# One DMA request moved forward in SyncE's program: the query and key weights of the attention steps

## Chip, cores, metric

The kernel runs on one core of one Trainium2 chip. The metric is device time in microseconds. Times are medians of several executions; every number about a single instruction is from one profiled execution.

## The reference, cut to what matters

The input is 1024 tokens of width 256 (2 sequences of 512). The output is x + A(xn) + F(xn), with xn the layer norm of x. A is a gated delta-rule attention with 16 key heads and 32 value heads. F is a causal softmax attention with 16 heads and then a mixture of 16 experts (4 chosen for each token) beside a shared expert. The change lies in F's softmax attention:

```python
x = rmsnorm(hidden_states, ln1_w)
q = jnp.einsum('bsh,dh->bsd', x, q_w).reshape(b, s, NH, QHD)[..., :NOPE]
kv = jnp.einsum('bsh,dh->bsd', x, kv_w)
k = kv[..., :NH * NOPE].reshape(b, s, NH, NOPE)
v = kv[..., NH * NOPE:NH * (NOPE + VD)].reshape(b, s, NH, VD)
scores = jnp.einsum('bqnd,bknd->bnqk', q, k) * scale
p = jax.nn.softmax(jnp.where(causal, scores, -1e9), axis=-1)
attn_out = jnp.einsum('bsd,hd->bsh', jnp.einsum('bnqk,bknd->bqnd', p, v).reshape(b, s, -1), o_w)
```

## The kernel before

The program has three stages, one after the other: F's attention (to about 500 us), the experts (to about 675 us), and A (the rest). Each engine has its own instruction list, and the engines meet at semaphores.

**The attention steps.** There are B * PAIRS = 16 steps, k = 0 to 15: 2 sequences times 8 pairs of heads. The weights of a step are three tiles, each with a single buffer: `wqk` (queries and keys, 512 KB), `wv` (values, 256 KB) and `wo` (output, 256 KB). TensorE works ahead by one step in part. Its order in step k is:

1. `project_v(k)` (L517), which reads `wv`. From its end on (`s_v` at 2k+2) `wv` is free.
2. `project_qk(k + 1, 0, 2)` (L502), the queries of the *next* step, for two heads. It waits for `s_ldq`, which the landing of `wqk` of step k+1 raises, and for the copies of the values out of PSUM (`s_vE`, DVE's `take_v`, L1459).
3. For i = 0 and 1: turn the probabilities (L594, waits for DVE's `s_prob`, L1622), then `project_qk(k + 1, 2 + i, 3 + i)`, the keys of the next step (L502 again). At the end of the second of them `s_qk` stands at 4(k+1)+4 and `wqk` is free.
4. Probabilities times values (L606), then `scores(k + 1, 0)` (L527).
5. The output projection (L628), which reads `wo` and raises `s_o`, then `scores(k + 1, 1)` (L527).

In steps 9, 10 and 12 some router work is put between (L535, L545, L553 to L559). Beside this DVE masks the scores, takes row maxima and scales the probabilities, and ScalarE exponentiates them and copies PSUM to SBUF.

**SyncE's list** asks for all transfers from memory and waits in order, so whatever stands behind a wait is late with it. In step k it waits for `s_qk` at 4k+4 and asks for `wqk` of step k+1 (L314), waits for `s_v` and asks for `wv` of step k+1 (L316), waits for `s_o` and asks for `wo` of step k+1 (L323), and then asks for the large transfers that the expert stage needs: in steps 0 to 7 two writes of zeros of 1 MB each to `xs_dram` (`clear_rows`, L305), in steps 8 to 15 the weights of one expert, 352 KB and 176 KB (`load_expert`, L308 and L309). In step 0 two stores of gate tables (L320) and a small write of zeros (L326) stand between. All of them go through one DMA queue.

Of the kernel before, what the change touches and what calls it, by code (L numbers as in the profile page):

```python
# [7 lines left out]
B, S, H = 2, 512, 256  # L8
# [14 lines left out]
PAIRS = NH // 2  # L23
# [20 lines left out]
def build(nc, d, out, debug=None):  # L44
# [9 lines left out]
    with ExitStack() as ctx:  # L54
# [3 lines left out]
        def sem(name):  # L58
            return ctx.enter_context(nc.semaphore(name))
# [16 lines left out]
        def early(name, shape, dt=F32):  # L76
            return early_ctx.enter_context(nc.sbuf_tensor(name, shape, dt))
# [32 lines left out]
        wqk = early("wqk", [P, 2, HK, 2 * P])  # L110
# [145 lines left out]
        sm = {n: sem(n) for n in names}  # L256
# [22 lines left out]
        def _(sp):  # L279
            dma = sp.dma_start  # L280
# [21 lines left out]
            def clear_rows(c):  # L302

                rows = xs_dram[c * CAP:(c + 1) * CAP].rearrange("(p m) h -> p m h", p=P)
                dma(rows, zeros[:].unsqueeze(1).broadcast_to([P, CAP // P, H])).then_inc(sm["m_zero"], 16)  # L305

            def load_expert(e):
                dma(we13[:, e, :], d["we13"][e].rearrange("p k n -> p (k n)")).then_inc(sm["m_we"], 16)  # L308
                dma(we2[0:IH, e, :], d["we2"][e].rearrange("p k n -> p (k n)")).then_inc(sm["m_we"], 16)  # L309

            for k in range(B * PAIRS):
                if k + 1 < B * PAIRS:
                    sp.wait_ge(sm["s_qk"], 4 * k + 4)
                    dma(wqk[:], d["wqk"][(k + 1) % PAIRS]).then_inc(sm["s_ldq"], 16)  # L314
                    sp.wait_ge(sm["s_v"], 2 * k + 2)
                    dma(wv[:], d["wv"][(k + 1) % PAIRS]).then_inc(sm["s_ldv"], 16)  # L316
                if k == 0:
                    sp.wait_ge(sm["s_gate_a"], 8)
                    for rows, table in ((grow_dram, growT), (erow_dram, erowT)):
                        dma(rows, table[:]).then_inc(sm["s_st"], 16)  # L320
                if k + 1 < B * PAIRS:
                    sp.wait_ge(sm["s_o"], 2 * k + 2)
                    dma(wo[:], d["wo"][(k + 1) % PAIRS]).then_inc(sm["s_ldo"], 16)  # L323
                if k == 0:
                    sp.wait_ge(sm["s_eps"], 3)
                    dma(xs_dram[E * CAP:], zeros[:]).then_inc(sm["m_zero"], 16)  # L326
                if k < 8:
                    clear_rows(2 * k)
                    clear_rows(2 * k + 1)
                else:  # L330
                    load_expert(k - 8)
# [1831 lines left out]
```

## Time and profile before

| | |
|---|---|
| median of 3 executions | 1696.54 us |
| lowest and highest of them | 1686.31 and 1699.68 us |
| the profiled execution, its own time | 1692.79 us |
| its span, from the first to the last instruction | 1691.0 us |
| mean granted TensorE clock | 0.966 |
| TensorE (PE) busy | 1556.0 us, 92% of the span |
| VectorE (DVE), ScalarE (ACT), GpSimd (POOL) busy | 1111.0, 785.5 and 438.8 us |
| moved by DMA | 136.88 MB, 81 GB/s on average |

The profile names an instruction by its line in the kernel. A busy TensorE says only that it had work, since a slower clock makes the same work last longer. A float32 matmul of 512 columns stands as two records. Consecutive matmul records overlap by about 0.16 us, so the length of a run of them is best taken from start to start. Names are cut to their common part: `we` holds the probabilities in DVE's and ScalarE's rows, and `act_t` holds keys, values and attention outputs.

### The profile page before, as it was taken

To read this page: it belongs to the slowest core of one execution; us is meant where nothing else is said; L and a number is where in the kernel's file an instruction comes from. 1 tells how busy PE (TensorE), PEld (TensorE's weight loads), DVE (VectorE), ACT (ScalarE), POOL (GpSimd) and SP (SyncE) were. 2 spreads that over 40 slices of the span, in tenths; PEclk is the share of its full clock that TensorE was granted. 3 is DMA by queue.
4 is the path that set the end of the run, shared out by engine and by line. 5 is a ranking of instruction groups with operands and counts; after the bars stand their busy time and mean duration, and the time that the engine had idled before them with its cause. 6 is when DMAs were issued, how large, how long until landed. Compare 5 with 4: busy or idle time off the path is not lost.

```text
span 1691.0 us, 29153 instructions
## 1 busy us (share of the span) xinstructions
PE 1556.0 (92%) x10922; PEld 1088.7 (64%) x10922; DVE 1111.0 (66%) x2442; ACT 785.5 (46%) x1692; POOL 438.8 (26%) x277
## 2 busy tenths in 40 slices
PE   5898889899997999659999999999999999999987
PEld 3556556566664676337776876776687677667756
DVE  4524324446536232377898898889888888988875
ACT  3433333434341333344665556465555646554641
POOL 0000000000304000523454263445415333531410
PEclk9999999999999899879999999999999999999999
DMA  2322322211333332513323331432333133233200
GB/s 94 103 75 85 140 75 98 90 60 55 125 86 99 107 107 79 142 50 69 98 62 80 91 87 49 103 97 62 79 83 79 41 94 86 57 67 84 59 10 32
DMA packets 225051, 136.88 MB, mean 81 GB/s; under 512 B 160976, under 2 KB 196304, under 8 KB 224912
## 3 DMA queue, kind: packets, MB, share of 16 engines
q1 hardware_dynamic: 221840, 126.62, 27.3%
q0 software_dynamic: 3072, 8.39, 1.5%
q8 instruction: 89, 1.46, 0.4%
q14 instruction: 50, 0.41, 0.1%
HBM read 94.85 MB, written 35.91 MB: 77 GB/s over the span
## 4 chain that ended last, share of the span: by engine, by line
PE 74%; issue 10%; DMA 6%; DVE 5%; SPq 2%; ACT 2%; POOL 1%; POOLq 1%; ACTq 0%; DVEq 0%
PE ps L502 7%; PE ps L909 7%; PE ps L808 7%; PE ps L827 6%; DMA wqk<-in_wqk 6%; PE ps L606 4%; PE ps L628 3%; PE ps L746 3%; PE ps L848 3%; PE ps L879 3%; PE ps L756 3%; PE ps L858 2%; PE ps L878 2%; PE ps L835 2%; PE ps L594 2%
## 5 line engine op out<-in xcount | busy, mean ns | idle before, releaser
L502 PE MATMUL ps<-xrT,wqk 128*128 128x512 f32 x256 | 134.8, 665 | 45.0 <-DMA wqk<-in_wqk 41.2
L1276 ACT ACTIVATE vs<-ps 128x256 f32<-128x256 f32 x128 | 49.2, 384 | 260.2 <-PE ps L848 256.0
L2024 POOL TENSOR_TENSOR qg<-qT,Ebc 128x1024 f32<-128x1024 f32 x32 | 75.0, 2364 | 357.1 <-PE ps L879 357.1
L1484 DVE TENSOR_TENSOR ps<-ps,causal_neg 128x128 f32<-128x128 f32 x128 | 37.4, 292 | 189.1 <-PE ps L527 189.1
L1701 DVE SCALAR_TENSOR_TENSOR cv<-ps,cw,cv 128x1022 f32<-128x1022 f32 (+2 forms) x96 | 122.6, 1279 | 28.1 <-ACT cv L1223 24.2
L808 PE MATMUL ps<-xnT,gv 128*128 128x512 f32 x256 | 121.7, 619 | 12.0 <-DVE cv L1701 11.5
L909 PE MATMUL ps<-wout,xT 128*128 128x256 f32 x512 | 128.8, 396 | 2.2 <-DVE total L1811 2.2
L1712 DVE SCALAR_TENSOR_TENSOR cv<-ps,cw,cv 128x1022 f32<-128x1022 f32 (+2 forms) x96 | 122.5, 1277 | 5.9 <-ACT cv L1255 3.6
L1811 DVE SCALAR_TENSOR_TENSOR total<-ps,rr,total 128x256 f32<-128x256 f32 x256 | 118.8, 480 | 10.0 <-POOL rr L2030 3.0
L827 PE MATMUL ps<-xnT,gz 128*128 128x512 f32 x256 | 121.1, 597 | 2.4 <-DVE MT L1745 2.2
L502 PEld LDWEIGHTS ps<-xrT,wqk 128*128 128x128 f32 x256 | 50.7, 213 | 100.4 <-issue 48.7
L1154 ACT ACTIVATE we<-ps,bias 128x128 f32<-128x128 f32 (+3 forms) x128 | 65.8, 526 | 106.0 <-DVE bias L1488 106.0
L909 PEld LDWEIGHTS ps<-wout,xT 128*128 128x128 f32 x512 | 93.3, 192 | 28.2 <-issue 12.6
L808 PEld LDWEIGHTS ps<-xnT,gv 128*128 128x128 f32 x256 | 47.5, 196 | 86.6 <-issue 73.6
L2008 POOL TENSOR_TENSOR dec<-dec,cb 128x1024 f32<-128x1024 f32 x32 | 60.1, 1898 | 166.3 <-DVE cb L1734 134.8
L1966 POOL TENSOR_SCALAR mean<-ssq 128x4 f32<-128x4 f32 x2 | 0.4, 192 | 362.9 <-ACT junk L1138 362.9
L879 PE MATMUL ps<-AT,vs 128*128 128x128 f32 x512 | 91.1, 275 | 0.0
L848 PEld LDWEIGHTS ps<-vs,PT 128*128 128x128 f32 x512 | 66.7, 194 | 26.1 <-issue 15.7
L1223 ACT ACTIVATE cv<-ps,cw 128x1024 f32<-128x1024 f32 x32 | 35.7, 1115 | 94.5 <-PE ps L756 62.0
L1994 POOL TENSOR_TENSOR dec<-dec,e_neg 128x1024 f32<-128x1024 f32 x32 | 75.4, 2377 | 16.1 <-DMA dec<-grow_dram 16.1
L878 PE MATMUL ps<-qg,St 128*128 128x128 f32 x384 | 74.4, 275 | 0.0
L527 PE MATMUL ps<-act_t,we 128*128 128x128 f32 (+3 forms) x256 | 74.3, 434 | 0.0
(256 smaller groups left out, 3581.4 us busy)
## 6 DMA issues: line engine op xcount, KB each, us to landing
xs_dram<-zeros SPq DMA_DIRECT2D x16, 1024.0 KB, 6.4
dec<-grow_dram SPq DMA_DIRECT2D x32, 512.0 KB, 4.8
Ebc<-erow_dram SPq DMA_DIRECT2D x32, 512.0 KB, 5.0
wqk<-in_wqk SPq DMA_DIRECT2D x16, 512.0 KB, 6.7
xn<-xs_dram SPq DMA_DIRECT2D x47, 128.0 KB, 2.0
ys_dram<-yg SPq DMA_DIRECT2D x47, 128.0 KB, 1.8
we<-in_we SPq DMA_DIRECT2D x16, 352.0 KB
wv<-in_wv SPq DMA_DIRECT2D x16, 256.0 KB, 4.6
```

The lines of the kernel that those rows point to most:

```text
L502: last = mm(ps[:, 6 + j % 2, :], wqk[:, i, c, w * P:(w + 1) * P], xrT[:, c, at:at + S], start=(c == 0), stop=(c == HK - 1))
L808: last = mm(ps[:, (Y, X)[r] + b, :], gv[:, k, r * D:(r + 1) * D], xnT[:, k, b * S:(b + 1) * S], start=(k == 0), stop=(k == HK - 1))
L827: last = mm(ps[:, X + b, :], gz[:, k, r * D:(r + 1) * D], xnT[:, k, b * S:(b + 1) * S], start=(k == 0), stop=(k == HK - 1))
L848: last = mm(ps[:, b, r * D:(r + 1) * D], PT[:, r * NT + 4 * b + m, :], vs[:, r, 4 * b + m, :], start=True, stop=True)
L878: mm(dst, St[:, m % 2, b * R + r, :], qg[:, r, t, :], start=True, stop=False)
L879: last = mm(dst, vs[:, r, t, :], AT[:, h % 2, r, t, :], start=(m == 0), stop=True)
L909: last = mm(ps[:, output_bank(t), r * H:(r + 1) * H], xT[:, r, t * P:(t + 1) * P], wout[:, r, :], start=True, stop=True)
L1701: ins = stt(row, pair(bank)[:, :, 0:S - k], cw[:, f, i, TAPS - 1 - k:TAPS - k], row, ALU.mult, ALU.add)
L1712: ins = stt(row, pair(bank)[:, :, 0:S - k], cw[:, n, 2 + r, TAPS - 1 - k:TAPS - k], row, ALU.mult, ALU.add)
L1811: ins = stt(total[:, t, :], ps[:, output_bank(t), r * H:(r + 1) * H], rr2[:, r, t:t + 1], total[:, t, :], ALU.mult, ALU.add)
L1994: tt(dec[:, r], dec[:, r], e_neg[:].unsqueeze(1).broadcast_to([P, NT, P]), ALU.add).then_inc(fl["g_self"], 1)
L2024: tt(qg[:, r], qT[:], Ebc[:, r], ALU.mult).then_inc(fl["g_qg"], 1)
```

## The change

SyncE asks for the `wqk` of step k+2 in step k, as soon as the last projection of step k+1 has read the buffer, ahead of its wait for `s_o`. The large expert transfers of a step now stand behind that request. The request for step 1 stands ahead of the loop. The same transfers are made, from the same engine, in another order; no other engine's list is touched.

```diff
+            sp.wait_ge(sm["s_qk"], 4)
+            dma(wqk[:], d["wqk"][1]).then_inc(sm["s_ldq"], 16)
             for k in range(B * PAIRS):
                 if k + 1 < B * PAIRS:
-                    sp.wait_ge(sm["s_qk"], 4 * k + 4)
-                    dma(wqk[:], d["wqk"][(k + 1) % PAIRS]).then_inc(sm["s_ldq"], 16)
                     sp.wait_ge(sm["s_v"], 2 * k + 2)
                     dma(wv[:], d["wv"][(k + 1) % PAIRS]).then_inc(sm["s_ldv"], 16)
+                if k + 2 < B * PAIRS:
+                    sp.wait_ge(sm["s_qk"], 4 * k + 8)
+                    dma(wqk[:], d["wqk"][(k + 2) % PAIRS]).then_inc(sm["s_ldq"], 16)
                 if k == 0:
                     sp.wait_ge(sm["s_gate_a"], 8)
                     for rows, table in ((grow_dram, growT), (erow_dram, erowT)):
```

## Rows read from the trace of the kernel before

**Rows 1.** The page's second part: granted TensorE clock in 40 slices of 42 us.
```profile
PEclk9999999999999899879999999999999999999999
```
**Rows 2.** TensorE's waits, first from 84 to 328 us, then from 328.5 to 485 us.
```profile
PE ps L502 <- DMA wqk<-in_wqk: 35.5, 8, 5.5
...
PE ps L502 <- DMA wqk<-in_wqk: 5.7, 6, 2.0
```
**Rows 3.** Timeline of TensorE in step 2, one of those with zero writes.
```profile
106.90 3.62 PE L517 MATMUL ps<-wv,xrT 128*128 128x256 f32 x16
114.53 5.40 PE L502 MATMUL ps<-xrT,wqk 128*128 128x512 f32 x8 [4.01 <-DMA wqk<-in_wqk]
119.76 1.25 PE L594 MATMUL ps<-ident,we 128*128 128x128 f32 x10
120.86 1.88 PE L502 MATMUL ps<-xrT,wqk 128*128 128x512 f32 x4
122.58 1.25 PE L594 MATMUL ps<-ident,we 128*128 128x128 f32 x10
...
131.86 3.62 PE L628 MATMUL ps<-wo,act_t 128*128 128x256 f32 x16
135.31 2.32 PE L527 MATMUL ps<-act_t,we 128*128 128x128 f32 x8
137.47 3.62 PE L517 MATMUL ps<-wv,xrT 128*128 128x256 f32 x16
```
**Rows 4.** TensorE, first and last value projection between which the stalls lie; later steps.
```profile
74.92 3.62 PE L517 MATMUL ps<-wv,xrT 128*128 128x256 f32 x16
...
340.09 1.04 PE L535 MATMUL ps<-ident,xn 128*128 128x128 f32 x8
...
366.60 1.86 PE L545 MATMUL ps<-wgate,xrT 128*128 128x16 f32 x16
...
419.94 0.79 PE L559 MATMUL ps<-keep,chunk_ones 128*128 128x48 f32 x6
...
436.25 3.70 PE L502 MATMUL ps<-xrT,wqk 128*128 128x512 f32 x8 [2.03 <-DMA wqk<-in_wqk]
...
483.21 3.62 PE L517 MATMUL ps<-wv,xrT 128*128 128x256 f32 x16
```
**Rows 5.** Timeline of SyncE's requests in one round: start, time to issue.
```profile
104.94 0.33 SPq L323 DMA_DIRECT2D wo<-in_wo  x1
105.31 1.26 SPq L305 DMA_DIRECT2D xs_dram<-zeros  x2
106.62 1.79 SPq L314 DMA_DIRECT2D wqk<-in_wqk  x1
110.55 0.33 SPq L316 DMA_DIRECT2D wv<-in_wv  x1
```
**Rows 6.** The chain that ended last: transfers of the weights in steps 2 and 13.
```profile
106.62 7.87 DMA wqk<-in_wqk
...
430.55 5.66 DMA wqk<-in_wqk
```
**Rows 7.** Groups by line and shape, 83 to 330 us: the projection's records.
```profile
L502 PE MATMUL ps<-xrT,wqk 128*128 128x512 f32 x131 | 76.8, 729 | 35.8 <-DMA wqk<-in_wqk 35.8
```
**Rows 8.** Windows of TensorE; of all engines in the last row. PEclk, DMA share and GB/s end each.
```profile
78.50:328.70 250.20, 214.45 (x801) 0.93 0.29 102
328.70:485.00 156.30, 150.90 (x625) 1.00 0.21 72
...
700.00:1650.00 950.00, 922.52 (x8287) 658.33 (x8284) 803.86 (x1638) 528.04 (x988) 380.20 (x218) 0.98 0.30 73
```
**Rows 9.** Timeline of DVE behind the value projection of step 14, which ends at 460.95.
```profile
461.15 0.69 DVE L1459 COPY act_t<-ps 128x512 f32<-128x512 f32 x1 [0.93 <-PE ps L517]
...
461.96 1.27 DVE L1622 TENSOR_SCALAR we<-we,prec 128x128 f32<-128x128 f32 x4
...
463.35 1.27 DVE L1622 TENSOR_SCALAR we<-we,prec 128x128 f32<-128x128 f32 x4
```

## The prediction

> **What bounds the kernel now.** I read the page first: TensorE is busy 92% of the span, so time can be won only where it idles or where its clock is low. The slices of the granted clock [rows 1] dip in slices 6 to 8, at about 210 to 335 us, inside the attention stage, and nowhere else below nine tenths. The table of waits then names the idle time of that stage: from step 1 on TensorE waits for one thing alone, the landing of `wqk`, 14 times, 35.5 us in eight waits of steps 1 to 8 and 5.7 us in six waits of steps 9 to 14 [rows 2]. Together that is 41.2 us.
>
> The timeline shows where. In step 2 the value projection starts at 106.90 and lasts 3.46 us (that is what the output projection of the same form takes from its start at 131.86 to the next start at 135.31), so TensorE is free at 110.36. It then stands still to 114.53, when `wqk` has landed [rows 3]. SyncE's list says why: `wqk` is asked for only at 106.62, behind `wo` and two zero writes of 1 MB, which were asked for at 104.94 and 105.31 [rows 5]. Its transfer then takes 7.87 us behind the zero writes, but 5.66 us behind one expert's weights [rows 6]. That is the difference between the two kinds of waits in [rows 2]. The chain that ended last runs through this transfer in each of these steps, so the wait is on the path.
>
> **Second cost of the wait: the clock.** The first projections behind a long wait are slow. Eight records of L502 need 5.23 us from start to start in step 2 (114.53 to 119.76), while four need 1.72 us a little later (120.86 to 122.58), so eight should need 3.44 us [rows 3]. In step 13, behind a wait of 2.03 us, the eight records are shown with 3.70 us instead of 5.40 [rows 3, 4]. The granted clock fits: 0.93 on average in steps 1 to 8, 1.00 in steps 9 to 14 [rows 8]. A mean of 0.93 is a mixture of the two levels, 2.4 and 1.2 GHz, and the lower one follows each wait of 4 us and more. The Trainium skill, "TensorE: Matmul & The Clock Gate", Part 1, says the same in general: the low clock is the default, and activity releases it; by that rule this cost goes with the wait.
>
> The sum of it comes from one row. From 83 to 330 us L502 has 131 records with 76.8 us of busy time [rows 7]: eight steps of 16 and three of the ninth. At full clock a step shows 3.60 + 1.88 + 1.88 = 7.36 us (3.44 plus the overlap of 0.16; 1.88 as in [rows 3]), so eight steps and three records (3 x 0.43 + 0.16) need 58.9 + 1.45 = 60.3 us. The low clock costs 76.8 - 60.3 = 16.5 us. In steps 9 to 14 the remainder (3.70 against 3.60) is 6 x 0.10 = 0.6 us.
>
> **The change, part by part.**
> - *The request for the next `wqk` moves ahead.* It now goes out when the last projection of step k+1 has read the buffer, which in step 2 would be about 125.4 (the L594 group that starts at 122.58 takes 1.10, and four records of L502 behind it 1.72). It is needed at the end of the next value projection, 137.47 + 3.46 = 140.93, so 15.5 us later [rows 3]. The transfer takes at most 7.87 us as shown, now with nothing large ahead of it. So at least 7 us are to spare, and all 14 waits go: 41.2 us, plus the overlap of 0.16 us that each wait row leaves out (110.36 is the true end, the row counts from 110.52), 2.2 us.
> - *The low clock behind the waits goes too*: 16.5 + 0.6 us.
> - *A new wait in SyncE's list* (`s_qk` at 4k+8). Queued behind it are the wait for `s_o` with `wo`, the zero writes or expert weights, and the next `wv`. The wait ends before L628 of the same step has even begun, and SyncE would have waited for L628 anyway, so none of them moves. In step 0 the two table stores of L320 come later within the step; they are read only in stage A. Cost 0; the lower bound is 0, since `wo` cannot go out before `s_o` in either kernel. The upper bound is one more issue of 1.79 us [rows 5] where nothing waits for it.
> - *`wv` is now the first request behind the zero writes.* It is asked for behind `s_v` (110.55, 5.2 us behind the first zero write) and is needed a full step later, some 24.6 us. Even with 7.87 us of transfer it has 16 us to spare. The skill's page "DMA: Bandwidth & Descriptors", section "Queues, rings and completion order", says that each DMA engine takes the descriptors of a ring in order, which makes `wv` the one that inherits the place of `wqk`; the rows here show that it can afford it.
> - *Zero writes and expert weights*: same requests, same place relative to L628. They come sooner in absolute time, as TensorE does.
>
> **What is late next.** Without the wait L594 follows 3.44 us behind L517. I take the slack from step 14, where L517 ends at 460.95. DVE copies the second half of the values until 461.84; the second projection needs it at 460.95 + 1.72 = 462.67: 0.8 us to spare. The first set of probabilities is scaled at 461.96 + 1.27 = 463.23, needed at 464.39: 1.16 us. The second is scaled at 464.62, needed at 467.21: 2.6 us [rows 9]. All three follow from the end of L517 and do not depend on the wait taken away, so no new wait comes up. The margin is thin, though, and it is the first thing to look at.
>
> **The sum, two ways.** By terms: 41.2 + 2.2 + 16.5 + 0.6 = 60.5 us. By periods: from the value projection of step 1 at 74.92 to that of step 15 at 483.21 are 408.3 us for 14 steps [rows 4]. A step without wait is 17.71 (119.76 to 137.47) + 3.46 + 3.44 = 24.6 us [rows 3], 14 of them 344.5; the router's pieces add 0.9 in step 9, 1.7 in step 10 and, with their two leading records, about 0.9 in step 12 [rows 4]. 408.3 - 344.5 - 3.5 = 60.3. Both agree. The later stages start from TensorE's own progress, so they shift as a whole.
>
> The profiled execution took 1692.79 us; less 60.4 is 1632.4. It is 3.75 us below the median of the runs shown, 1696.54. Against that median the forecast is 1636. The lower clock in those waits may be part of the spread from 1686.31 to 1699.68, so the result may lie a little lower.
>
> **Rivals.**
> - *Softmax takes over the wait.* DVE's chain is late by more than its 1.16 us. For: the slack is small, and DVE's times are from one execution. Against: it is the same chain to a hundredth in steps with and without long waits. If it were 1.4 us later than needed in 14 steps, 20 us would be lost: 1656. Chance 0.05.
> - *The slow projections come from the zero writes, not from the idle time before them.* Steps 1 to 8 have both, and steps 9 to 14 neither, so rows alone do not separate them. Against: the granted clock is low just there, and in step 2 the later L502 records are at full speed. Only the waits would go, 43.4 us: 1653. Chance 0.05.
> - *The request does not do what it says*: `wqk` still lands late, or `wv` or `wo` does in its place. At the price of the waits of steps 9 to 14 (5.7 us in six, about 1 us each) 14 us stay: 1650. All margins above speak against it. Chance 0.04.
> - *Slower: denser work draws the clock down.* TensorE would be busy without a gap for 345 us. If the granted clock fell for it, and stayed down in the rest, the loss would exceed 60 us from a mean fall of about 4% over the some 1500 us of busy time that follow; at 0.93, the mean of steps 1 to 8, it is 1500 x 0.07 = 105 us, so 1741. Against: stage A runs at 0.98 with 97% busy for 950 us, and steps 9 to 14 at 1.00 with 97% [rows 8]. The same page of the skill on TensorE knows such a limiter, but only once three cores of a die work densely; here it is one. Chance 0.02.
> - *The full gain*: 1636. Chance 0.84.
>
> **How the numbers follow.** The likeliest case alone spans 1627 to 1645: the runs before lie 10 us below and 3 us above their median, and the terms are good to some 3 us. To take in the near edge of the first three rivals I go to 1650. About 1% (17 us) is what a measurement of this kernel can tell from no change; all but the slower case, and a remainder of 0.02 for a mixture of losses, are faster by more than that: faster 0.96, same 0.02, slower 0.02.
>
> **What would show it.** In the profile after: no wait of L502 for `wqk` in steps 1 to 14; L502 near 0.43 us a record in all steps; clock 1.00 from about 80 to 425 us; 14 steps in about 348 us; SyncE's request for `wqk` between those for `wv` and `wo`, landing in well under 7.87 us; the time of stage A unchanged. The prediction is wrong if L594 now waits for DVE L1622, if L502 waits for `act_t` copies (L1459), or if the slow records stay where zeros are being written.

## The result, and the profile after

The changed kernel takes 1628.6 us (median of 4, 1627.9 to 1631.3) against 1698.1 us before (median of 4, 1686.3 to 1704.1): a ratio of 0.961, 95% interval 0.958 to 0.965. Timed again on another occasion it was 1631.4 against 1693.7 us: 0.963, interval 0.960 to 0.966. The profiled execution took 1629.19 us, its span is 1627.4 us.

TensorE's waits in the attention stage after the change, from 60 to 480 us. The wait of L502 for `wqk` [rows 2] is gone from the list; L502 is now L505, and every line behind the edit has moved by three.

```profile
PE ps L597 <- DVE we L1625: 2.3, 1, 2.3
PE ps L631 <- ACT act_t L1169: 0.8, 1, 0.8
```

Both rows belong to step 15, which projects nothing ahead, and both stood there before. The timeline of TensorE in step 2, against [rows 3]:

```profile
101.14 3.62 PE L520 MATMUL ps<-wv,xrT 128*128 128x256 f32 x16
104.59 3.60 PE L505 MATMUL ps<-xrT,wqk 128*128 128x512 f32 x8
...
125.73 3.62 PE L520 MATMUL ps<-wv,xrT 128*128 128x256 f32 x16
```

The eight records of L505 follow the value projection at once and take 3.43 us from start to start (the next group, L597, starts at 108.02), and the step takes 125.73 - 101.14 = 24.59 us. SyncE's list in the same stretch, against [rows 5]:

```profile
99.17 0.33 SPq L326 DMA_DIRECT2D wo<-in_wo  x1
99.54 1.27 SPq L305 DMA_DIRECT2D xs_dram<-zeros  x2
104.78 0.33 SPq L316 DMA_DIRECT2D wv<-in_wv  x1
113.84 0.33 SPq L319 DMA_DIRECT2D wqk<-in_wqk  x1
```

The request for `wqk` at 113.84 has nothing large ahead of it, and its transfer takes 3.6 us (median), where it was 7.9 in steps 1 to 8 and 4.5 to 5.7 in steps 9 to 14. `wv` stands next behind the zero writes and lands in 3.3 us (median). The records of the projection from 60 to 520 us as a group, by line and shape, against [rows 7]:

```profile
L505 PE MATMUL ps<-xrT,wqk 128*128 128x512 f32 x232 | 106.8, 592 | 0.0
```

One record is shown with 592 ns on average, where it was 729 in steps 1 to 8. A window of TensorE, against [rows 8], over the stretch of the stalls, from the value projection of step 1 to that of step 15:

```profile
76.54:424.42 347.88, 347.88 (x1433) 1.00 0.32 105
```

TensorE is busy for every microsecond of it, at full clock. Before, the same stretch took 408.29 us [rows 4]. So 60.41 us of the 63.6 us between the two spans are won there. In front of it stand 76.54 us (74.92 before), behind it 1202.98 us (1207.79 before); the next section shows that such parts vary by 2 to 3 us without any edit.

### The profile page after: what moved, and what is told of

Same layout as the page of the kernel before. It is cut to its first block, busy times and chain, and to the rows that moved or that the text cites. A ratio compares the mean times of both kernels' runs of the same rounds, so it can differ in the third digit from the quotient of the medians.

```text
span 1627.4 us, 29153 instructions
## 1 busy us (share of the span) xinstructions
PE 1534.4 (94%) x10922; PEld 1081.3 (66%) x10922; DVE 1111.6 (68%) x2442; ACT 784.7 (48%) x1692; POOL 438.4 (27%) x277
## 4 chain that ended last, share of the span: by engine, by line
PE 80%; issue 10%; DVE 5%; ACT 2%; POOL 1%; DMA 1%; POOLq 1%; SPq 0%; ACTq 0%; DVEq 0%
PE ps L912 7%; PE ps L811 7%; PE ps L505 6%; PE ps L830 6%; PE ps L609 4%; PE ps L530 4%; PE ps L631 3%; PE ps L520 3%; PE ps L749 3%; PE ps L851 3%; PE ps L882 3%; PE ps L759 3%; PE ps L861 2%; PE ps L881 2%; PE ps L838 2%
## 5 line engine op out<-in xcount | busy, mean ns | idle before, releaser
L505 PE MATMUL ps<-xrT,wqk 128*128 128x512 f32 x256 | 119.5, 601 | 3.6 <-ACT we L1116 2.8
L505 PEld LDWEIGHTS ps<-xrT,wqk 128*128 128x128 f32 x256 | 46.7, 193 | 45.9 <-issue 40.3
L1782 DVE SCALAR_TENSOR_TENSOR St<-St,eg,ps 128x128 f32<-128x128 f32 x128 | 35.9, 342 | 57.0 <-PE ps L861 57.0
```

Source lines behind the costliest of these rows:

```text
L505: last = mm(ps[:, 6 + j % 2, :], wqk[:, i, c, w * P:(w + 1) * P], xrT[:, c, at:at + S], start=(c == 0), stop=(c == HK - 1))
```

## The experiments

The measure used throughout is the stretch between the value projections of steps 1 and 15, "the 14 steps", since it leaves out what the rest of the program does from run to run. All kernels of one group were run on the same chip, with the kernel before beside them.

**Both kernels once more (before_again, after_again).** No edit. Where does the spread lie, and is there a gain outside the 14 steps?

> The kernel before, unchanged, for the spread of its time and for a second profile. Theory 1 (the spread of 18 us sits in the attention steps, in the length of the waits for the weights and of the low clock behind them): between the value projections of step 1 and step 15 this profile differs from 408.3 us by several us, and the rest of the span by less. Theory 2 (the spread sits in the later stages): 408.3 within 2 us, the rest differs. Time 1686 to 1704.

> The changed kernel, unchanged, timed once more on one chip against the kernel before. Theory 1 (all that is won are the 60.4 us between the value projections of steps 1 and 15, and the rest of the first measurement's 66 us is spread): ratio 1 - 60.4/1692 = 0.964, 1631 to 1632. Theory 2 (a further gain in the later stages): ratio 0.961, 1626.

before_again: 1692.16 us (1688.1 to 1695.6, 10 runs), ratio 0.9997 to the kernel before (0.998 to 1.001). Value projections of steps 1 and 15:

```profile
76.54 3.62 PE L517 MATMUL ps<-wv,xrT 128*128 128x256 f32 x16
...
484.42 3.62 PE L517 MATMUL ps<-wv,xrT 128*128 128x256 f32 x16
```

The 14 steps take 407.88 us against 408.29, the rest behind them 1204.58 against 1207.79. after_again: 347.89 us against 347.88, the rest 1204.94 against 1202.98. This is as theory 2 had it for before_again and theory 1 for after_again: in these two profiles the steps repeat to 0.4 us, the later stages vary by 2 to 3 us in either kernel, and no gain in them shows beyond that. The two profiled executions of the kernel before lie only 2 us apart, so they say nothing of an execution at either end of its spread. The first measurement's ratio of 0.961 holds some of that spread; 1 - 60.4/1692 = 0.9643 lies in both intervals.

**The order alone (asked_behind_wo).** The changed kernel, with the request no longer early, only ahead of the large transfers:

```diff
-                if k + 2 < B * PAIRS:
-                    sp.wait_ge(sm["s_qk"], 4 * k + 8)
-                    dma(wqk[:], d["wqk"][(k + 2) % PAIRS]).then_inc(sm["s_ldq"], 16)
...
                     dma(wo[:], d["wo"][(k + 1) % PAIRS]).then_inc(sm["s_ldo"], 16)
...
+                if k + 2 < B * PAIRS:
+                    sp.wait_ge(sm["s_qk"], 4 * k + 8)
+                    dma(wqk[:], d["wqk"][(k + 2) % PAIRS]).then_inc(sm["s_ldq"], 16)
                 if k < 8:
                     clear_rows(2 * k)
```

> The changed kernel, with the request for the query and key weights of step k+2 only behind that for wo in step k, but still ahead of the large expert transfers: only the order is changed, the request is not early. It goes out 0.4 us behind the output projection and is needed 5.6 us behind it. Theory A (the place behind the large transfers was the whole cost): a transfer of about 4 us, waits of 0 to 0.3 us, full clock, within 4 us of the changed kernel, about 1630. Theory B (the request must be early as well): waits of about 1 us as in steps 9 to 14 of the kernel before, full clock, about 14 us above the changed kernel, 1643.

1635.8 us, ratio 0.965 (0.963 to 0.968). The waits of TensorE for the weights, 60 to 560 us (steps 1, 6, 8 and 13):

```profile
PE ps L505 <- DMA wqk<-in_wqk: 2.9, 4, 1.0
```

The 14 steps take 351.87 us. Of 60.4 us, 56.4 come with the order alone; the early request adds the last 4.0, of which 2.9 are these four waits. What the order gives has two parts. The transfer is shorter, 4.2 us (median) against 7.9 in steps 1 to 8. And SyncE no longer spends 1.3 us on issuing the zero writes first: it asks for the weights 0.4 us behind `wo` and not 1.7 us behind it [rows 5]. Theory A was right on the cause and a little low on the time: the transfers fit on average into their allowance of 5.2 us, but single ones take more, 5.66 us in step 6 and 6.15 us in step 13. That is the part that only the early request makes safe.

**Half of the zeros ahead (one_zero_write_ahead).** The kernel before, with the second zero write behind the weights:

```diff
                     dma(wqk[:], d["wqk"][(k + 1) % PAIRS]).then_inc(sm["s_ldq"], 16)
+                    if 1 <= k <= 8:
+                        clear_rows(2 * k - 1)
...
                     clear_rows(2 * k)
-                    clear_rows(2 * k + 1)
```

> The kernel before, with the second zero write of steps 0 to 7 asked for behind the query and key weights, so that 1 MB stands ahead of them and not 2 MB; steps 8 to 15 as before. All theories expect the waits of steps 1 to 8 to fall from 4 to 5 us to about 0.5 to 1 us (35.5 us to 4 to 8). Idle theory (the slow projections come from the idle time before them): with waits this short the clock stays full though zeros are still being written, and 16.5 us more are won: 1698 less 45 is 1653. Zero-write theory (the slow projections come from zeros in flight): only the waits are won: 1698 less 29 is 1669.

1660.4 us, ratio 0.979 (0.977 to 0.982), between the 1653 us of the one theory and the 1669 us of the other. The time alone decides nothing, since the waits of steps 1 to 8 fell by 18 us only, from 35.5 to 17.5. The 14 steps take 377.64 us. Two of them on TensorE's timeline:

```profile
86.59 3.70 PE L503 MATMUL ps<-xrT,wqk 128*128 128x512 f32 x8 [2.93 <-DMA wqk<-in_wqk]
...
194.06 5.40 PE L503 MATMUL ps<-xrT,wqk 128*128 128x512 f32 x8 [2.37 <-DMA wqk<-in_wqk]
```

The waits of steps 1 to 8 are 1.6 to 2.9 us and not 0.5 to 1: a transfer behind one zero write takes 6.0 to 7.1 us, so the megabyte taken away is worth some 2 us and not 3 to 4. On the clock the kernel speaks for the idle theory: each of these steps has zero writes ahead of and behind the weights, and six of eight have full clock. Two are slow, behind waits of 2.37 and 2.52 us, while one of 2.93 us is not. The cost of a wait of that length is thus not fixed.

A look at what the DMA engines do *while* the eight records run says more, in the kernel before too, where the trace could have answered the question without a run. The first window is step 2 of the kernel before, the second the step of this kernel that starts at 86.59. The three numbers at the end are the granted clock, the DMA share and GB/s:

```profile
114.53:119.76 5.23, 5.23 (x8) 0.67 0.02 6
...
86.59:90.10 3.51, 3.51 (x8) 1.00 0.85 309
```

In all eight slow steps of the kernel before at most 7 GB/s move during the slow records, so nothing large is in flight any more once the weights have landed; the granted clock there is 0.53 to 0.68. The other window has heavy traffic and full clock. So a transfer in flight at the same time is not what slows the records. What this leaves of the zero-write theory is a clock lowered by the zeros that were written during the wait, and the next kernel takes these away.

**The wait without the zeros (late_without_zeros_near).** The kernel before, with the weights asked for late and the large transfers in the middle of the step:

```diff
                 if k + 1 < B * PAIRS:
-                    sp.wait_ge(sm["s_qk"], 4 * k + 4)
+                    sp.wait_ge(sm["s_v"], 2 * k + 2)
                     dma(wqk[:], d["wqk"][(k + 1) % PAIRS]).then_inc(sm["s_ldq"], 16)
-                    sp.wait_ge(sm["s_v"], 2 * k + 2)
                     dma(wv[:], d["wv"][(k + 1) % PAIRS]).then_inc(sm["s_ldv"], 16)
+                    sp.wait_ge(sm["s_qk"], 4 * k + 8)
+                if k < 8:
+                    if k:
+                        clear_rows(2 * k)
+                        clear_rows(2 * k + 1)
+                else:
+                    load_expert(k - 8)
...
-                if k < 8:
-                    clear_rows(2 * k)
-                    clear_rows(2 * k + 1)
-                else:
-                    load_expert(k - 8)
+                if k == 0:
+                    clear_rows(0)
+                    clear_rows(1)
```

> The kernel before, with the request for the query and key weights held back to the end of the value projection, ahead of wv, and the large transfers moved to the middle of the step (behind the last key projection), so that the wait stays but nothing large is in flight at it (step 0 keeps its zero writes at the end). All expect waits of 3.7 to 4.3 us in each of the 14 steps. Idle theory: each is followed by slow projections, 1.7 us or more a step, 14 x (4.1 + 2.0) = 85 us above the changed kernel, about 1714, slower than before. Zero-write theory: full clock behind the waits, 14 x 4.1 = 57 us above, about 1686.

1714.2 us, ratio 1.012 (1.009 to 1.015), as the idle theory had it. The wait, summed over the steps, from 60 to 560 us:

```profile
PE ps L506 <- DMA wqk<-in_wqk: 56.6, 14, 5.4
```

Two of the steps on TensorE's timeline, and the window of the second (granted clock, DMA share and GB/s at its end):

```profile
204.34 3.70 PE L506 MATMUL ps<-xrT,wqk 128*128 128x512 f32 x8 [3.73 <-DMA wqk<-in_wqk]
...
420.42 5.40 PE L506 MATMUL ps<-xrT,wqk 128*128 128x512 f32 x8 [3.74 <-DMA wqk<-in_wqk]
...
420.42:425.66 5.24, 5.24 (x9) 0.67 0.01 4
```

The median transfer is 3.7 us with nothing large near (only step 1 has zeros ahead of its weights, those of step 0). 13 of 14 waits are followed by slow projections, in steps 9 to 14 too, where the kernel before had none. The 14 steps take 431.46 us, 83.6 above the changed kernel: 56.6 + 14 x 0.16 of waits, and 24.7 of low clock, 1.9 on average in each slow step. Together with the changed kernel, which writes the same zeros in the same steps at clock 1.00, this settles it: the low clock comes with the idle time, not with the zeros.

**How near is the next wait (softmax_pad_small, softmax_pad_large).** The changed kernel, with 3 or 9 useless DVE instructions a step behind the copy of the values:

```diff
                     take_v(k)
+                    for i in range(9):
+                        dve.tensor_reduce(pad[:, i:i + 1], causal_neg[:], AX.X, ALU.max)
```

> The changed kernel with three more DVE instructions a step (row maxima of a constant 128x128 tile into a tile that nothing reads) between the copy of the values and the scaling of the probabilities, some 0.8 us by the rows of L1486 (0.29 us one, a little less from start to start). Theory A (1.16 us of slack in front of the probabilities, as read from the trace before): no wait in steps 1 to 14, and only step 15, where TensorE waits for DVE anyway, is 0.8 us longer: +1 us. Theory B (the slack is gone, softmax is the next bound): 15 x 0.8 = +12 us.

> The same with nine such instructions, some 2.4 us. Theory A: each of steps 1 to 14 waits for the probabilities for 2.4 - 1.16 = 1.2 us, 17 us, and step 15 is 2.4 us longer: +20 us, with full clock as the waits are short. Theory B: 15 x 2.4 = +36 us. If DVE is nowhere near the path: +2 us.

The small pad: 1631.5 us beside 1631.4 of the unpadded kernel on the same chip; the 14 steps take 347.89 us, the same to 0.01. The large pad: 1644.9 us, 13.5 more than the unpadded kernel where theory A had 20; the 14 steps take 358.57 us. Its timeline in step 3, DVE's pad and TensorE's wait for what follows it:

```profile
129.94 1.82 DVE L1618 TENSOR_REDUCE pad<-causal_neg 128x1 f32<-128x128 f32 x9
131.67 0.17 DVE L1623 RECIPROCAL prec<-psums 128x4 f32<-128x4 f32 x1
...
133.30 1.28 PE L598 MATMUL ps<-ident,we 128*128 128x128 f32 x10 [0.57 <-DVE we L1628]
```

Nine instructions take 131.67 - 129.94 = 1.73 us and not 2.4, since they follow one another every 0.19 us. Each step is longer by (358.57 - 347.89)/14 = 0.76 us, so the slack is 1.73 - 0.76 = 0.97 us. Theory A holds, with a slack of 0.97 where 1.16 had been read from the trace. The scaling that starts at 131.88 ends 1.27 us later, at 133.15, and TensorE starts at 133.30: these 0.15 us from DVE's end to TensorE's start are most of the difference. The small pad adds 0.58 us and leaves some 0.4 us of the slack.

**Does what stands behind a transfer slow it (second_zero_write_far, behind_wo_large_far, zeros_far_experts_near)?** The waits of one_zero_write_ahead had come out too long, and I asked whether the transfer behind the weights was to blame. The first takes one_zero_write_ahead and moves the second zero write behind `wv`. The second takes asked_behind_wo and moves all large transfers of step k-1 there (the lines that they leave at the end of the step, and the last expert's request behind the loop, are not shown):

```diff
                     dma(wv[:], d["wv"][(k + 1) % PAIRS]).then_inc(sm["s_ldv"], 16)
+                if 1 <= k <= 8:
+                    clear_rows(2 * k - 2)
+                    clear_rows(2 * k - 1)
+                elif k > 8:
+                    load_expert(k - 9)
```

The third, zeros_far_experts_near, has only the zero writes there.

> The kernel before, with one zero write of steps 0 to 7 ahead of the query and key weights as in one_zero_write_ahead, but the other one asked for only behind wv, when the weights have landed, so that nothing large stands behind them. Steps 8 to 15 as before. Serial theory (a transfer waits only for what was asked for ahead of it): the transfer takes 7.1 us and the waits of steps 2 to 8 are 1.6 to 2.5 us, as in one_zero_write_ahead, 1660. Sharing theory (what is asked for behind it takes bandwidth from it as well): the transfer takes about 5 us, the waits 0 to 0.5 us, low clock nowhere in steps 2 to 8, 1645.

> asked_behind_wo (the request for the weights of step k+2 only behind that for wo), with the large transfers moved behind the request for wv of the next step, so that they are neither ahead of nor behind the weights in flight. Sharing theory: a transfer of 3.6 to 4 us, no wait, the time of the changed kernel, 1628 to 1632. Serial theory: the large transfers never stood ahead of the weights there, so 1635 as asked_behind_wo, with transfers of 4.2 us and single waits of 0.5 to 1 us.

second_zero_write_far: 1665.1 us, ratio 0.981 (0.978 to 0.985). The weights in step 3, from the chain that ended last:

```profile
128.18 6.56 DMA wqk<-in_wqk
```

The transfers of steps 2 to 5 take 5.97, 6.56, 6.03 and 6.01 us, against 6.16, 7.08, 6.13 and 6.95 us in one_zero_write_ahead. That is 0.4 us less on average (0.3 over all eight steps), not 2. The sharing theory falls as the main cause: a transfer waits for what was asked for ahead of it, and what stands behind it costs it little. The 5 us that I had assumed for a transfer behind one megabyte were simply too short. The kernel is not faster than one_zero_write_ahead, though its waits are shorter: its step 13 takes 33.15 us, 8.6 more than a step without a wait, as told next.

behind_wo_large_far took 1642.8 us, ratio 0.967 (0.964 to 0.970), more than either theory had. It waits for the weights once, 0.3 us, but loses 8.3 us in step 13. Its timeline there, GpSimd, SyncE, DVE and TensorE:

```profile
383.92 0.96 POOL L1981 DMA_INDIRECT xs_dram<-xn,place  x1 [0.30 <-issue]
384.37 0.33 SPq L316 DMA_DIRECT2D wv<-in_wv  x1
384.38 0.69 DVE L1463 COPY act_t<-ps 128x512 f32<-128x512 f32 x1 [6.42 <-remote]
...
385.12 3.78 PE L506 MATMUL ps<-xrT,wqk 128*128 128x512 f32 x4 [4.53 <-DVE act_t L1463]
```

The value projection's second half shows as over at about 378.1, and TensorE itself goes on at 378.61, but SyncE and DVE, which both wait for the semaphore of that half, go on only at 384.4. GpSimd issues its indirect transfers, which send rows, about every 1.3 us throughout. second_zero_write_far, on the same chip, has such a gap in the same step. Two more kernels asked what it hangs on:

> behind_wo_large_far with the expert transfers of steps 8 to 15 back behind the weights at the end of the step; only the zero writes stay behind wv. It asks where the 8 us in step 13 of behind_wo_large_far are from, where the value projection's semaphore came 6 us late to SyncE and DVE while GpSimd was sending rows. If they hang on the place of the expert transfers, step 13 is back to a wait of at most 1 us as in asked_behind_wo, and the time is 1630 to 1633. If not, step 13 is long here too, 1640. In steps 1 to 8 no wait but that of step 6 (0.3 us).

> behind_wo_large_far unchanged, for a second profile: if the 8 us of step 13 belong to the program, they stand there again; if they were a chance of that execution, step 13 takes 24.6 to 25.6 us.

zeros_far_experts_near: 1633.4 us, ratio 0.967 (0.963 to 0.970), the 14 steps 351.24 us, with a wait for the weights of 2.07 us in step 13, longer than the 1 us expected, but no such gap. behind_wo_large_far_again, the same program on another occasion: 1633.36 us, the 14 steps 349.48 us, step 13 with a wait of 0.85 us and no such gap. So the 8 us are not a fixed part of the program. They are hardly the chance of one execution either: all four of behind_wo_large_far on the first occasion took 1640.3 to 1643.3 us. The second occasion was another chip and a single execution, so whether the gap hangs on the chip or on the moment, and what it is, stays open. In all kernels that ask for the weights late, step 13, in which GpSimd sends rows, has one of the longer waits of steps 9 to 14 (2.03 in the kernel before, 1.98 in its second profile).

None of these kernels beats the changed one: 347.9 us for the 14 steps is what TensorE's own work takes.

## Why the prediction was right

Forecast were 1636 us, 60.4 us below the median of 1696.54 us. Measured were 1628.6 and 1631.4 us, and 60.41 us in the stretch where the gain was placed.

- *What bounds the kernel*: right, by the table of waits [rows 2]. With the wait gone nothing else came up in its place. The reading of [rows 1] was wrong: the lower digits there are the 14th, 17th and 18th of the 40, at about 550 to 590 and 675 to 760 us, in and just behind the expert stage. The slices of the attention stage all show 9, since its mean of 0.93 is still over nine tenths. The low clock of the steps shows in [rows 3] and [rows 8], and its term in the sum was taken from [rows 7], so the sum took no harm.
- *The waits go*: right, all 14. 15.5 us of allowance for `wqk` are ample: 3.6 us are used. The 7.87 us taken as the longest transfer were not the longest; that of step 3 took 8.35 us in the kernel before, which the allowance covers as well.
- *The low clock goes too*: right as a separate term of some 17 us. The rival, that the zero writes slow the projections, was left open by the rows shown, but not by the trace: in step 2 the DMA engines move 6 GB/s during the slow records. It is ruled out by the changed kernel (zeros, no wait, full clock) and by late_without_zeros_near (waits, no zeros, low clock).
- *The new wait in SyncE's list costs nothing, and `wv` can afford its place*: right. Neither `wo` nor `wv` appears among TensorE's waits, and `wv` lands faster than before, in 3.3 us against 4.6; that `wqk` no longer stands just ahead of it is the likely reason.
- *What is late next*: right, the scaling of the probabilities, with 0.97 us of slack measured by padding where 1.16 was read. Of the difference 0.15 us is the time from DVE's end to TensorE's start, which reading ends of one engine against starts of another leaves out.
- *Sum by periods*: 14 steps in 348.0 us forecast, 347.88 and 347.89 measured.
- *The offset to the median*: this was the weak step. I added the 3.75 us by which the profiled execution lay below the median of three, and supposed that the spread of the kernel before sat partly in its waits. Nothing here supports that: the steps repeat to 0.4 us in two profiles, and on one chip the changed kernel, which has no such wait, spreads over 7.8 us (five executions) where the kernel before spreads over 9.0 us (nine). The medians of the kernel before on the several occasions were 1691.4 to 1699.2 us, so a median of three is no firmer base than the profiled execution itself. 1632.4 would have been the better number here. That 1628.6 us lie nearer to it than to 1636 is in part luck, since the rest of the program took some us less in that execution for no reason of the change.
- *Denser work draws the clock down*: it did not; 1.00 over 348 us without a gap, and the stages behind took 1203.0 and 1204.9 us, against 1207.8 and 1204.6 before.

The cause by parts is now also known: the order ahead of the large transfers is worth 56.4 us, the earlier request 4.0 us.

## What to carry to other kernels

A wait for a small transfer is often a wait for the large ones asked for ahead of it on the same queue; before looking for bandwidth, put what is needed first ahead of what is needed last, and then ask early enough that a single slow transfer does not matter. Price a recurring wait of TensorE with the slow work behind it: here 4 us of idle time cost some 2 us more. To ask whether a transfer slows an engine, first look at what the DMA engines move while its slow instructions run. When the wait is gone, the slack of the next one can be read off by comparing its ends with the new start, and a few useless instructions measure it.

## What the runs showed of the hardware that was not expected

- Waits of nearly one length fall on both sides: a wait of 3.73 us left the clock full and one of 3.74 us did not, and 2.37 us lowered it where 2.93 us did not. None of the waits of up to 2.07 us lowered it, some 40 in all these kernels. The shortest that did is shown as 2.13 us, in step 13 of second_zero_write_far (granted clock 0.56 behind it).
- A transfer of 512 KB took 3.7 us with nothing large near, 6.0 to 7.1 us with one megabyte of zeros asked for just ahead, and 7.9 us behind two; large transfers asked for behind it cost some 0.4 us.
- On one chip, and in two programs, a matmul's semaphore reached SyncE and DVE 6 to 8 us late while GpSimd was issuing indirect transfers. One of the two programs on another chip showed nothing of the kind. The cause is open.
